# Row maxima kept whole in fp32, and key-major attention scores divided by head parity, in an audio tower on one NeuronCore

## The reference, cut to what matters

```python
h = _L0_tok_ref(x, ...)                       # (32, 64, 256)
# attention of _layernorm(h):
q = jnp.einsum('bshd,ed->bshe', xh, Wq)       # k, v alike
energy = jnp.einsum('bqhd,bkhd->bhqk', q, k) / jnp.sqrt(jnp.float32(e))
attn = jax.nn.softmax(energy, axis=-1)
out = jnp.einsum('bhqk,bkhd->bqhd', attn, v).reshape(b, s, e)
h = h + out @ W_out.T + b_out
h = h + _L0_ffn_ref(_layernorm(h, axis=-1), ...)
```

## Time and profile before

| | |
|---|---|
| three runs | 142.89, 143.12, 143.40 us; median 143.12 |
| the profiled execution | 143.03 us, with a span of 141.2 us from first to last instruction |
| mean granted TensorE clock | 0.991 |
| busy: TensorE matmul, loads | 133.0 us, 112.7 us |
| busy: VectorE, ScalarE, GpSimd | 111.9, 86.1, 94.9 us |
| one step in the middle | 5.59 us |

### The profile page before, as it was taken

The page is one execution under the profiler, slowest core; times in us unless marked ns, Lnnn a source line. Parts: engine busy times, 40 slices in busy tenths (PEclk is TensorE's granted clock), DMA queues, the critical chain, the costliest instruction groups (busy, mean ns, idle before and its releaser), DMA issues.

```text
span 141.2 us, 6132 instructions
## 1 busy us (share of the span) xinstructions
PE 133.0 (94%) x2444; PEld 112.7 (80%) x2444; DVE 111.9 (79%) x337; ACT 86.1 (61%) x245; POOL 94.9 (67%) x186
## 2 busy tenths in 40 slices
PE   6879999999999998999999999999999999999861
PEld 2469999999988786888878879889788788788540
DVE  4684596869978578798898898988988988978751
ACT  4375675478878585865946847648558477455110
POOL 3284797996583374678687687696876876773361
PEclk9999999999999999999999999999999999999996
DMA  4678000030000010121311302203113123031102
GB/s 71 156 169 264 10 0 0 0 38 11 0 0 5 5 19 6 18 51 14 63 38 23 60 28 33 59 6 63 48 13 60 37 23 59 7 59 42 37 0 74
DMA packets 24508, 5.89 MB, mean 42 GB/s; under 512 B 20384, under 2 KB 24224, under 8 KB 24480
## 3 DMA queue, kind: packets, MB, share of 16 engines
q1 hardware_dynamic: 24192, 5.37, 18.3%
q10 hardware_dynamic: 288, 0.13, 0.3%
HBM read 2.35 MB, written 2.10 MB: 32 GB/s over the span
## 4 chain that ended last, share of the span: by engine, by line
PE 79%; DVE 7%; POOL 4%; issue 3%; DMA 3%; ACT 1%; SPq 1%; POOLq 0%; DVEq 0%
PE bank L1037 11%; PE bank L954 11%; PE bank L1023 7%; PE bank L1100 6%; PE bank L1076 5%; PE bank L959 5%; PE bank L1081 4%; PE bank L1121 4%; PE bank L1065 3%; DMA wf_raw<-in_W_r 3%; PE bank L1050 2%; PE bank L1134 2%; PE bank L948 2%; PE bank L1104 2%; PE bank L1125 2%
## 5 line engine op out<-in xcount | busy, mean ns | idle before, releaser
L824 DVE TENSOR_REDUCE bank<-bank 128x4 f32<-128x256 f32 x64 | 22.8, 425 | 7.3 <-ACT pT L376 6.9
L376 ACT ACTIVATE pT<-bank 128x256 f32<-128x256 f32 x64 | 19.4, 389 | 2.6 <-PE bank L1050 2.6
L1037 PE MATMUL bank<-qT,xzT 32*128 32x64 f32 x512 | 17.9, 276 | 0.0
L1037 PEld LDWEIGHTS bank<-qT,xzT 32*128 32x128 f32 x512 | 15.7, 186 | 2.7 <-issue 2.7
L695 DVE TENSOR_TENSOR hid_lo<-bank,hid_hi 128x512 fp32r<-128x512 f32 x16 | 11.0, 686 | 7.3 <-ACT bank L344 7.3
L582 POOL TENSOR_TENSOR side_lo<-sideT,side_hi 128x256 fp32r<-128x256 f32 x14 | 10.2, 730 | 8.4 <-ACT sideT L386 8.4
L545 POOL TENSOR_SCALAR xblk<-xh,parity_sb 128x128 f32<-128x128 f32 x32 | 11.6, 375 | 6.0 <-PE bank L1081 4.9
L371 ACT ACTIVATE maxT<-bank 128x128 fp32r<-128x128 f32 x16 | 4.4, 278 | 17.8 <-PE bank L1059 17.8
L593 POOL TENSOR_TENSOR on_lo<-onT,on_hi 128x256 fp32r<-128x256 f32 x14 | 10.3, 736 | 7.1 <-ACT on_hi L390 6.9
L553 POOL TENSOR_TENSOR hb_all<-h_all,bout_bc 128x256 f32<-128x256 f32 x16 | 11.6, 738 | 4.1 <-ACT h_all L348 4.1
L361 ACT ACTIVATE xzT<-bank,parity_sb 128x256 f32<-128x256 f32 x28 | 12.0, 497 | 0.0
(11 more groups left out here) (166 smaller groups left out, 387.2 us busy)
## 6 DMA issues: line engine op xcount, KB each, us to landing
out<-y SPq DMA_DIRECT2D x16, 128.0 KB, 1.7
xblk<-xh SPq DMA_DIRECT2D x32, 32.0 KB, 2.5
wo_raw<-in_W_o SPq DMA_DIRECT2D x1, 512.0 KB, 4.0
wout_raw<-in_W_out SPq DMA_DIRECT2D x1, 256.0 KB, 3.1
fr<-in_wr SPq DMA_DIRECT2D x1, 256.0 KB, 4.1
fi<-in_wi SPq DMA_DIRECT2D x1, 256.0 KB, 4.2
minus_raw<-in_minus_rows SPq DMA_DIRECT2D x1, 128.0 KB, 2.2
bout_bc<-in_b_out SPq DMA_DIRECT2D x1, 128.0 KB, 3.9
```

Source lines behind the costliest of these rows:

```text
L376: nc.scalar.activation(pT[:, j, :], bank[j][:, D:2 * D], ACT.Exp).then_inc(exp_done, 1)
L824: nc.vector.tensor_reduce(rowmax[:, j, :], bank[j][:, 0:D].rearrange("p (h k) -> p h k", k=TOK), AX_X, ALU.max).then_inc(max_done, 1)
L1037: pe.matmul(bank[j][:, at0:at0 + TOK], xzT[t % 3][rows32, 2 * half + b, :, :].rearrange("p e k -> p (e k)"), qT[t % 3][rows32, half, TOK * ...
```

## The change

The maxima stay whole. `maximum` writes them straight into `max_rows` in SBUF (four of every 32 columns, the rest zero), `split_max` is gone, with its two semaphores and `rowmax`, and `turn_max` waits for the four maxima. `maxT` and `minus_rows` become fp32, the table is loaded where it is used (`minus_raw`, the GpSimd copy and `minus_set` are gone), and it picks one row per head instead of two.

`take_max` is cut by head parity e into products of 64 weight columns, 16 instead of 8, each into 64 of the 128 output partitions. `keyed_scores` is cut in the same way, 32 products instead of 16, with e outside j.

```diff
-    minus_rows = np.where((r[:, None, None] % 32 < 8) & (r[:, None, None] % 4 == head_of[None]), -1.0, 0.0).astype(np.float32)
+    minus_rows = np.where(r[:, None, None] % 32 == head_of[None], -1.0, 0.0).astype(np.float32)
...
-        minus_raw = sb("minus_raw", [P, HALF, P])
-        minus_rows = sb("minus_rows_sb", [P, HALF, P], F32R)
+        minus_rows = sb("minus_rows_sb", [P, HALF, P])
...
-        max_terms = sb("max_terms", [P, QUADS, 32], F32R)
-        maxT = sb("maxT", [P, P], F32R)
+        max_rows = sb("max_rows", [P, QUADS, 32])
+        maxT = sb("maxT", [P, P])
...
-            sp.dma_start(minus_raw[:], a["minus_rows"]).then_inc(att_loaded, 16)
+            sp.dma_start(minus_rows[:], a["minus_rows"]).then_inc(att_loaded, 16)
...
-            nc.gpsimd.tensor_copy(minus_rows[:], minus_raw[:]).then_inc(minus_set, 1)
...
-                nc.vector.tensor_reduce(rowmax[:, j, :], bank[j][:, 0:D].rearrange("p (h k) -> p h k", k=TOK),
+                nc.vector.tensor_reduce(max_rows[:, j, 0:4], bank[j][:, 0:D].rearrange("p (h k) -> p h k", k=TOK),
                                         AX_X, ALU.max).then_inc(max_done, 1)
-
-            def split_max(t):
-                dve.wait_ge(max_done, QUADS * (t + 1))
-                if t >= 1:
-                    dve.wait_ge(max_turned, t)
-                nc.vector.tensor_copy(max_terms[:, :, 0:4], rowmax).then_inc(max_hi_set, 1)
-                dve.wait_ge(max_hi_set, t + 1)
-                nc.vector.tensor_tensor(max_terms[:, :, 4:8], rowmax, max_terms[:, :, 0:4].bitcast(F32),
-                                        ALU.subtract).then_inc(max_lo_set, 1)
...
                 for half in range(HALF):
                     for b in range(2):
+                        for e in range(2):
+                            for j in range(QUADS):
+                                rows32 = slice(32 * j, 32 * j + 32)
+                                at0 = D + half * P + TOK * b
+                                pe.matmul(bank[j][TOK * e:TOK * e + TOK, at0:at0 + TOK],
+                                          xzT[t % 3][rows32, 2 * half + b, e, :],
+                                          qT[t % 3][rows32, half, TOK * b:TOK * b + TOK],
+                                          start=(half == 0 and b == 0), stop=False, skip_group_check=True)
+
+            def take_max(t):
+
+                pe.wait_ge(max_copied, t + 1)
+                if t == 0:
+                    pe.wait_ge(att_loaded, 64)
+                for half in range(HALF):
+                    for e in range(2):
                         for j in range(QUADS):
                             rows32 = slice(32 * j, 32 * j + 32)
-                            at0 = D + half * P + TOK * b
-                            pe.matmul(bank[j][:, at0:at0 + TOK],
-                                      xzT[t % 3][rows32, 2 * half + b, :, :].rearrange("p e k -> p (e k)"),
-                                      qT[t % 3][rows32, half, TOK * b:TOK * b + TOK],
-                                      start=(half == 0 and b == 0), stop=False, skip_group_check=True)
...
-                        last = pe.matmul(bank[j][:, D + half * P:D + (half + 1) * P], minus_rows[rows32, half, :],
-                                         maxT[rows32, :], start=False, stop=(half == HALF - 1), skip_group_check=True)
-                        if half == HALF - 1:
-                            last.then_inc(keyed_done, 1)
+                            last = pe.matmul(bank[j][TOK * e:TOK * e + TOK, D + half * P:D + (half + 1) * P],
+                                             minus_rows[rows32, half, TOK * e:TOK * e + TOK], maxT[rows32, :],
+                                             start=False, stop=(half == HALF - 1), skip_group_check=True)
+                            if half == HALF - 1 and e == 1:
+                                last.then_inc(keyed_done, 1)
...
             def turn_max(t):
-                pe.wait_ge(max_lo_set, t + 1)
+                pe.wait_ge(max_done, QUADS * (t + 1))
```

More of the change, by code:

```diff
@@ L171, in audio_tower_kernel @@
         FREQ_BANK, SIDE_BANK, QUERY_BANK = PROJ_BANK, MAX_BANK, X_BANK
-        rowmax = bank[MAX_BANK][:, P:P + 4 * QUADS].rearrange("p (j h) -> p j h", h=4)
         bh_loaded, br_loaded = sem("bh_loaded"), sem("br_loaded")
@@ L199, in audio_tower_kernel @@
         halfway_measured, halfway_averaged = sem("halfway_measured"), sem("halfway_averaged")
-        minus_set = sem("minus_set")
         hi_done, lo_done, wo_split = sem("hi_done"), sem("lo_done"), sem("wo_split")
@@ L215, in audio_tower_kernel @@
             sem("scores_done"), sem("max_done"), sem("max_turned"), sem("max_copied"))
-        max_hi_set, max_lo_set = sem("max_hi_set"), sem("max_lo_set")
         keyed_done, exp_done = sem("keyed_done"), sem("exp_done")
@@ L646, in _ @@
                 nc.vector.memset(xblk[i][:], 0.0).then_inc(zeros_set, 1)
-            nc.vector.memset(max_terms[:].bitcast(F32), 0.0).then_inc(zeros_set, 1)
+            nc.vector.memset(max_rows[:], 0.0).then_inc(zeros_set, 1)
             def place_wh(part, src):
@@ L887, in step @@
                         maximum(i + 2, j)
-                    split_max(i + 2)
                 if i < T:
@@ L896, in _ @@
                 maximum(0, j)
-            split_max(0)
             split_x(2)
@@ L904, in _ @@
                 maximum(1, j)
-            split_max(1)
             mean_shift(3)
@@ L1033, in keyed_scores @@
                     for b in range(2):
-                        for j in range(QUADS):
-                            rows32 = slice(32 * j, 32 * j + 32)
-                            at0 = D + half * P + TOK * b
-                            pe.matmul(bank[j][:, at0:at0 + TOK],
-                                      xzT[t % 3][rows32, 2 * half + b, :, :].rearrange("p e k -> p (e k)"),
-                                      qT[t % 3][rows32, half, TOK * b:TOK * b + TOK],
-                                      start=(half == 0 and b == 0), stop=False, skip_group_check=True)
+                        for e in range(2):
[6 more added lines that the diff above has]
+                                          start=(half == 0 and b == 0), stop=False, skip_group_check=True)
             def take_max(t):
@@ L1045, in take_max @@
                 if t == 0:
-                    pe.wait_ge(minus_set, 1)
+                    pe.wait_ge(att_loaded, 64)
                 for half in range(HALF):
-                    for j in range(QUADS):
-                        rows32 = slice(32 * j, 32 * j + 32)
-                        last = pe.matmul(bank[j][:, D + half * P:D + (half + 1) * P], minus_rows[rows32, half, :],
-                                         maxT[rows32, :], start=False, stop=(half == HALF - 1), skip_group_check=True)
-                        if half == HALF - 1:
-                            last.then_inc(keyed_done, 1)
+                    for e in range(2):
+                        for j in range(QUADS):
+                            rows32 = slice(32 * j, 32 * j + 32)
+                            last = pe.matmul(bank[j][TOK * e:TOK * e + TOK, D + half * P:D + (half + 1) * P],
[3 more added lines that the diff above has]
+                                last.then_inc(keyed_done, 1)
             def turn_max(t):
-                pe.wait_ge(max_lo_set, t + 1)
+                pe.wait_ge(max_done, QUADS * (t + 1))
                 if t == 0:
                     pe.wait_ge(h_copied, T - 1)
-                pe.transpose(bank[MAX_BANK][:, 0:P], max_terms[:].rearrange("p j r -> p (j r)").bitcast(F32),
+                pe.transpose(bank[MAX_BANK][:, 0:P], max_rows[:].rearrange("p j r -> p (j r)"),
                              ident[:]).then_inc(max_turned, 1)
```

## The result

| | before | after |
|---|---|---|
| median | 143.00 us (4 runs beside it) | 151.45 us (4 runs, 151.03 to 152.10) |
| ratio, 95% interval | | 1.058 (1.0558 to 1.0603) |
| span of the profiled execution | 141.2 us | 149.5 us |
| mean granted TensorE clock | 0.991 | 0.992 |

The account below looks back on a forecast made before the run. TensorE, busy 94% of 141.2 us, was taken as the bound. Eleven steps at 0.19 (2.1 us), 0.37 for the next step, 0.37 for the first key-major stage and 0.41 for the residual: 143.03 - 3.3 = 139.7 us, range 137.5 to 143.0.

Parts of the forecast that it names:

- 8 x 56 = 0.45 us instead of 0.90: Key-major stage on TensorE: each of eight places has 8 records, each a 56 ns load under a 56 ns stream.
- eight places run at once: Key-major scores: four row groups, each split by head parity, work in parallel, as the scores L1023 already showed.
- the third rival: TensorE's dense stages: a floor per record, 14 ns giving about 143.7 us; 0.20 together with loads sharing a path.
- the shared loads: Column halves of a 32-row group share a load path, 143.8 us; 0.20 together with a floor of 14 ns or more.
- Scores: Stage L1023 on TensorE, already in the divided shape: 0.45 us in the sum of three stages.
- the pause ahead of the key-major scores: TensorE's "issue" wait at the tile shape change before L1037: it goes, about 0.2 us from last stream to first load.
- subtraction and drain: Subtraction of the maxima on TensorE: 0.45 us instead of 0.22, plus 0.2 for the shape change ahead of L1100.
- The path over ScalarE and GpSimd: From transposed maxima to xh: next bound, 5.40 us per step instead of 5.59, so 0.19 of 0.37 us arrives.
- The first residual without its split: TensorE's wait for the residual at 55.48 us, ahead of the steady steps, goes: 0.41 us gained.
- Maxima into SBUF at nothing: VectorE writing maxima to SBUF instead of PSUM: the same 0.42 us, so 0 taken.
- Rival 2: Halves share a load path: three stages 2.00 us, 0.08 more per step, 143.8 us; 0.20 with floors of 14 ns upward.
- The estimate of 25 ns per record: All 96 records of the three stages: 60 cycles each, 2.4 us, some 158 us; chance 0.02 of the slower cases.

Follow-up runs that it names:

- the one-term kernel: The kernel before without the split of the maxima, subtracting one rounded fp32r term over 128 columns; 142.42 us, ratio 0.9954.

## Why the prediction was wrong

The sum failed in one term and lacked another.

**The mis-sized term: the key-major scores, "8 x 56 = 0.45 us instead of 0.90".** Measured 0.80 to 0.87. I read the old stage's 0.91 as time for loading 128 columns, and took half of it for half of the columns, as if the number of records cost nothing. With 32 columns the stage doesn't fall, with half the pairs it does. That eight places run at once was right, but TensorE came near such a pace only in the first half of the last stage (32 pairs in 0.29 us). What I needed stood in the third rival: the densest row has a pair every 14 ns, and the new stage has 64 pairs. By that rival the stage is 64 x 14 ns = 0.90 us and the kernel 143.7; the kernel with 64 instructions more, less its gaps, is at 143.7. As a sum it was right, though no single pair has this floor. I gave that case and the shared loads 0.20 together, although no row showed a whole stage at a denser pace.

**The term that was missing: the supply of instructions, 6.5 us.** The sum priced records by what they do and none by their number. Neither the forecast nor a rival had a wait that depends on how many instructions TensorE consumes in a stretch. Step by step the rest held:

- Scores 0.49 for 0.45; the pause ahead of the key-major scores gone; subtraction and drain 0.66 for 0.45 + 0.2. Right.
- The path over ScalarE and GpSimd at 5.40 us per step: right, though not in this kernel, whose TensorE stayed slower. Where TensorE was made faster, in four kernels, the steps came to 5.38 to 5.49, but for two of 5.57 and 5.76.
- The first residual without its split, 0.41 us: the one-term kernel gained 0.49. In the changed kernel the wait is gone too, but TensorE comes to it 0.43 us later, so the residual is taken up at 55.45 and the gain is lost.
- Maxima into SBUF at nothing: 416 ns for 425, right.
- Rival 2 had the right sign and size for the steps (0.08 more each) by a wrong mechanism.

The estimate of 25 ns per record in the prediction, from the Trainium skill, "TensorEngine Tiling (Array Packing)", section "Instruction Overhead", is not borne out by the pace either: the pairs of these stages come every 12 to 15 ns. That its 158 us was nearer to the result than mine is an accident of the gaps.

## What to carry to other kernels

A product that is cut in two for more parallel places has twice the records: price it by the number of its pairs, at the pace of the densest whole stage in the trace, before pricing it by columns. Then count TensorE's loads and matmuls in the densest microseconds: where 256 were used up in 2.3 to 2.6 us this kernel ran out of program, and kernels with 176 to 192 in their dense stretch did not in the steady loop. The sign is "issue" time in the middle of a uniform stage, at instruction numbers a multiple of 256 apart. A value that cancels later needs no exactness; saving its terms and records was worth 2.6% here.

## What was unexpected of the hardware

Packets of q8 took 1.0 to 1.6 us ahead of the eight gaps, and TensorE went on 1.2 to 1.5 us after they had landed; the packet began 0.4 to 1.4 us after the first instruction of the block then running. The three add up to more than the block lasted (2.3 to 2.6 us, 3.65 ahead of the last gap), and the rest is the gap. The Trainium skill, "Runtime: NRT & Kernel Launch", section "Instruction fetch mechanics", says that an engine's program comes in blocks of 16 KiB, 256 instructions, over a DMA queue of its own, the next one being fetched while one runs; packets and record numbers here agree. It also says that crossing into a new block is mostly hidden. In the kernel before the trace agrees, with no such gap in its steady loop; in the changed kernel it does not, with up to 1.44 us at a crossing and 6.5 us in all. What makes a packet begin early or late, and so a gap of 0.34 or of 1.44 us, stays open: no run changed the traffic of the other queues.
